# A two-layer recurrence on one core: three of layer 1's four tiles in bf16 parts, its columns in two halves, residual sums on GpSimd

## The chip, the cores and the metric

The kernel runs on one core of a Trainium2 chip. Its time is the device time of one execution in microseconds; the median of 3 runs before the change is 2182.97 us (2181.4 to 2183.67). All matrices and the input and output lie in HBM at the start and the end.

## The reference

```python
def layer(x, h0, Wx, Wh, b):              # N=8 rows, T=1024 steps, 512 columns
    xW = jnp.einsum('ntd,dh->nth', x, Wx) + b
    def step(h_prev, xw_t):
        h_next = jnp.tanh(h_prev @ Wh + xw_t)
        return (h_next, h_next)
    _, hs = jax.lax.scan(step, h0, jnp.swapaxes(xW, 0, 1))
    return jnp.swapaxes(hs, 0, 1)

x = x + layer(x, cond, L0_Wx, L0_Wh, L0_b)   # float32 throughout
x = x + layer(x, cond, L1_Wx, L1_Wh, L1_b)
```

Each layer is a chain of 1024 steps, each step a product of an 8x512 state with a 512x512 matrix, a sum with the projected input of that step, and a tanh. Layer 1 reads layer 0's output.

## The kernel before, in words

The 512 state columns are four tiles k of 128 partitions. A matmul has a state tile as its stationary operand, 32 columns wide (four steps' places of 8 rows, of which the current step's is filled and the others are zero), and 128 columns of the weight as its moving operand. The four column tiles g of the array take the four 128-column pieces of the weight, so a product with one k is a set of four matmuls, and its result stands as 32 rows per g in one PSUM bank.

Layer 0's step (recur0, L221) is 4 k x 4 g = 16 fp32 calls. Layer 1's (recur1) has two kinds of product. Tiles 2 and 3 are fp32 calls (L238). Tiles 0 and 1 (KB = 2) are exact sums of bf16 parts (L249): the weight is split once into three bf16 parts (wh_part, made on GpSimd), the state every step into three that lie in three of the tile's places (rest, L405, twice a step). The places' rows are added after the product by total1. The projections (L210) of both layers are done four steps at a time, and their 8 products per four steps are laid between the recurrences by the table PROJECT, two a step.

A step's way round: TensorE finishes a bank and increments rec_done; VectorE transposes it (turn0 L387, turn1 L391), in layer 1 also sums the places (total1 L397); ScalarE's tanh writes the new state (tanh0 L324, tanh1 L331); in layer 1 VectorE then splits it (L405). ScalarE also copies the projected input into the bank in which the next step of layer 1 accumulates (begin1, L313) and the bias into the projections' banks (L306). Layer 1 runs LAG = 8 steps behind layer 0, and in each slot TensorE does recur0, a projection, recur1, a projection. The residual sums sum_mid (L420, x plus layer 0's output, which layer 1's projection reads) and sum_out (L425) run on VectorE once in four slots.

The order of the work is the order in which each engine's program is written. VectorE's, ScalarE's, GpSimd's and SyncE's programs are unrolled over all slots. TensorE's is written as turns of RING = 8 slots: two turns unrolled (FIRST = 2), then one turn as the body of a hardware loop (Fori) of 125 passes, then three unrolled turns. Semaphores count up over groups of four slots and are set back, so that the loop's body waits for the same numbers in each pass.

Of the kernel before, what the change touches and what calls it, by code (L numbers as in the profile page):

```python
# [15 lines left out]
KB = 2  # L16
# [6 lines left out]
NG = T // S4  # L23
DMA = 16
# [3 lines left out]
WARM = 8  # L28
# [12 lines left out]
ORDER = [(l, n) for s in range(T + LAG) for l in LAYERS if (n := number(l, s)) is not None]  # L41
# [9 lines left out]
def build(nc, x, h_init, weights, out):  # L51
    ctx = ExitStack()
    with ctx:  # L53
# [3 lines left out]
        def psum(name):  # L57
            return ctx.enter_context(nc.psum_tensor(name, [P, 512], F32))
# [27 lines left out]
        ps_rec1 = [psum(f"ps_rec1_{i}") for i in range(2)]  # L86
# [40 lines left out]
        def h_count(l, n):  # L127

            s = n + LAG * l
            steps = [(m, t) for t in range(s - s % S4, s + 1) for m in LAYERS  # L130
                     if number(m, t) is not None and (m, number(m, t)) != (0, T - 1)]
            return h_done[s // S4 % 2], steps.index((l, s)) + 1

        def split_count(n):

            s = n + LAG
            return split_done[s // S4 % 2], s % S4 + 1
# [63 lines left out]
        def _(pe):  # L201
# [23 lines left out]

            def recur1(n):

                bank = ps_rec1[n % 2]  # L230
# [49 lines left out]
            for i in range(WARM):  # L280
                for bank in (*ps0, *ps_xw1, *ps_rec1):
# [20 lines left out]
        def _(act):  # L302
# [5 lines left out]
            def begin1(n):  # L308
# [4 lines left out]
                act.activation(ps_rec1[n % 2][:, 0:P], ps_xw1[c % 2][:, 0:P], ACT.Copy,  # L313
# [13 lines left out]
            def tanh1(n):  # L327
                if n % S4 == 0 and n // S4 + 1 < NG:
                    act.wait_ge(mid_done, n // S4 + 2)
                act.wait_ge(z1_done, n + 1)  # L330
                act.activation(h_of(1, n), z1[n % 2][:, :].rearrange("p (k b) -> p k b", k=KC), ACT.Tanh).then_inc(  # L331
                    h_count(1, n)[0], 1)

            def slot(s):
                last = None
                for l in LAYERS:
                    if (m := number(l, s - 1)) is not None and (l, m) != (0, T - 1):
                        last = (l, m)
# [32 lines left out]
        def _(pool):  # L371
            pool.dma_start(h_first[:, :], h_init).then_inc(s_first, DMA)
# [5 lines left out]
            pool.tensor_copy(wh_part[:, 0, :], upper(full)).then_inc(s_wpart, 1)  # L378
            pool.wait_ge(s_wrest, 1)
            pool.tensor_copy(wh_part[:, 1, :], upper(rest)).then_inc(s_wpart, 1)  # L380
            pool.tensor_tensor(wh_part[:, 2, :], rest, upper(rest), ALU.subtract).then_inc(s_wpart, 1)

        @block.vector
        def _(dve):
            def turn0(n):
                dve.wait_ge(rec_done, STEP_AT[0, n])
                dve.transpose(zt[0][n % 2][:, :], ps0[n // S4 % 2][:, 0:P]).then_inc(zt0_done, 1)  # L387

            def turn1(n):
                dve.wait_ge(rec_done, STEP_AT[1, n])  # L390
                dve.transpose(zt[1][n % 2][:, :], ps_rec1[n % 2][:, 0:P]).then_inc(zt1_done, 1)  # L391

            def total1(n):

                at = LOWEST[n % S4] * B
                dve.wait_ge(zt1_done, n + 1)
# [93 lines left out]
```

## Time and profile before

| | |
|---|---|
| median of 3 runs | 2182.97 us |
| profiled execution, its time | 2181.98 us |
| its span, first to last instruction | 2180.2 us |
| TensorE matmuls busy | 2157.1 us (99%), 90304 of them |
| VectorE busy | 1306.2 us (60%) |
| ScalarE busy | 807.7 us (37%) |
| GpSimd busy | 8.6 us (0%) |
| mean granted TensorE clock | 0.997 |

PE is TensorE's matmuls and PEld its weight loads, DVE is VectorE, ACT ScalarE, POOL GpSimd. An L number is a line of the kernel above. "issue" is idle time for which the profile shows no wait. In a view of busy time by stretch, the number behind the x in brackets counts the instructions that ran in the stretch. The granted clock is a fraction of 2.4 GHz. q1, q8 and q14 are DMA queues; those that are called "instruction" carry the engines' programs.

### The profile page before, as it was taken

The numbers are of one execution on the slowest core, as the hardware profiler recorded it, in microseconds if no ns is written. First come the engines' busy times: TensorE is split into PE (matmuls) and PEld (weight loads), VectorE is DVE, ScalarE is ACT, GpSimd is POOL, SyncE is SP. The second block draws the span as 40 slices with busy tenths as digits, with TensorE's granted clock in tenths as the row PEclk, the third lists the DMA queues.
The fourth block names the chain that finished last, engine by engine and source line by source line (L and its number), as shares of the span: only waits on it lengthen the run. The fifth ranks groups of instructions, "written<-read, shape, count | busy, mean of one in ns | idle before, by whom it ended". The sixth has DMA issues, their size and how long they took to land.

```text
span 2180.2 us, 192439 instructions
## 1 busy us (share of the span) xinstructions
PE 2157.1 (99%) x90304; PEld 2127.9 (98%) x90304; DVE 1306.2 (60%) x5643; ACT 807.7 (37%) x3585; POOL 8.6 (0%) x11
## 2 busy tenths in 40 slices
PE   7999999999999999999999999999999999999997
PEld 7999999999999999999999999999999999999997
DVE  3566666666666666666666666666666666666665
ACT  2333333333333333333333333333333333333333
POOL 1000000000000000000000000000000000000000
PEclk9999999999999999999999999999999999999999
DMA  3000000000000000000000000000000000000000
GB/s 101 23 26 22 26 22 26 22 26 22 26 22 26 22 26 22 26 22 26 22 26 22 26 22 26 22 25 23 24 23 25 23 25 23 24 24 23 25 22 17
DMA packets 112033, 55.84 MB, mean 26 GB/s; under 512 B 12448, under 2 KB 111024, under 8 KB 111536
## 3 DMA queue, kind: packets, MB, share of 16 engines
q1 hardware_dynamic: 111456, 53.53, 8.5%
q10 hardware_dynamic: 432, 1.18, 0.1%
q14 instruction: 90, 0.74, 0.1%
q8 instruction: 23, 0.38, 0.1%
q0 software_dynamic: 32, 0.02, 0.0%
HBM read 37.90 MB, written 16.78 MB: 25 GB/s over the span
## 4 chain that ended last, share of the span: by engine, by line
PE 99%; DVE 0%; DMA 0%; issue 0%; ACT 0%; SPq 0%; DVEq 0%; ACTq 0%
PE ps L221 41%; PE ps_rec L238 21%; PE ps_rec L249 16%; PE ps L210 10%; PE ps_xw L210 10%; DMA wx<-wx_in 0%; DVE zt L391 0%; DVE z L397 0%; ACT h L331 0%; DVE zt L387 0%; ACT h L324 0%; SPq L180 0%; SPq L178 0%; DVE h L405 0%; DVEq L53 0%
## 5 line engine op out<-in xcount | busy, mean ns | idle before, releaser
L221 PE MATMUL ps<-wh,h 128*32 128x128 f32 x32768 | 1089.6, 273 | 4.9 <-ACT h L324 2.8
L221 PEld LDWEIGHTS ps<-wh,h 128*32 128x32 f32 x32768 | 907.9, 110 | 22.9 <-ACT h L324 5.1
L238 PE MATMUL ps_rec<-wh,h 128*32 128x128 f32 x16384 | 638.8, 273 | 7.8 <-ACT h L331 7.1
L391 DVE STREAM_TRANSPOSE zt<-ps_rec 128x128 f32<-128x128 f32 x1024 | 324.6, 317 | 423.2 <-PE ps_rec L249 417.0
L405 DVE TENSOR_TENSOR h<-h 128x16 f32<-128x16 f32 x2050 | 359.4, 175 | 354.4 <-ACT h L331 319.1
L249 PE MATMUL ps_rec<-wh_part,h 128*32 128x128 bf16 x24576 | 534.2, 219 | 0.9 <-issue 0.8
L324 ACT ACTIVATE h<-zt 128x32 f32<-128x32 f32 x1024 | 235.1, 230 | 725.1 <-DVE zt L387 725.1
L238 PEld LDWEIGHTS ps_rec<-wh,h 128*32 128x32 f32 x16384 | 463.1, 110 | 14.8 <-ACT h L331 13.4
L331 ACT ACTIVATE h<-z 128x32 f32<-128x32 f32 x1024 | 235.1, 230 | 637.4 <-DVE z L397 637.4
L249 PEld LDWEIGHTS ps_rec<-wh_part,h 128*32 128x32 bf16 x24576 | 460.2, 97 | 2.7 <-issue 1.6
L210 PE MATMUL ps<-wx,x_pe 128*32 128x128 f32 x8192 | 414.7, 273 | 4.8 <-ACT ps L306 3.0
L210 PE MATMUL ps_xw<-wx,x_mid 128*32 128x128 f32 x8192 | 413.7, 273 | 0.0
L313 ACT ACTIVATE ps_rec<-ps_xw,mask 128x128 f32<-128x128 f32 x1024 | 330.2, 322 | 0.0
L387 DVE STREAM_TRANSPOSE zt<-ps 128x128 f32<-128x128 f32 x1024 | 316.2, 309 | 20.9 <-PE ps L221 20.9
L397 DVE TENSOR_REDUCE z<-zt 128x32 f32<-128x96 f32 x1024 | 271.7, 265 | 34.9
L210 PEld LDWEIGHTS ps<-wx,x_pe 128*32 128x32 f32 x8192 | 219.9, 110 | 6.6 <-issue 4.3
L210 PEld LDWEIGHTS ps_xw<-wx,x_mid 128*32 128x32 f32 x8192 | 220.0, 110 | 0.3 <-issue 0.3
L420 DVE TENSOR_TENSOR x_mid<-x_dve,h 128x128 f32<-128x128 f32 x256 | 74.8, 292 | 32.1 <-DVE x_out L425 7.3
L306 ACT ACTIVATE ps_xw<-bias 128x128 f32<-128x128 f32 x256 | 69.4, 271 | 0.0
L306 ACT ACTIVATE ps<-bias 128x128 f32<-128x128 f32 x256 | 67.4, 264 | 0.3
L425 DVE TENSOR_TENSOR x_out<-x_mid,h 128x128 f32<-128x128 f32 x256 | 63.9, 250 | 0.0
L283 PE MATMUL ps<-zeros 128*32 128x128 bf16 x64 | 3.1, 288 | 1.0 <-DVE zeros L444 1.0
(21 smaller groups left out, 22.7 us busy)
## 6 DMA issues: line engine op xcount, KB each, us to landing
x_pe<-x_t SPq DMA_DIRECT2D x256, 64.0 KB, 2.0
x_dve<-x_t SPq DMA_DIRECT2D x256, 64.0 KB, 2.0
out_t<-x_out SPq DMA_DIRECT2D x256, 64.0 KB, 1.5
wx<-wx_in SPq DMA_DIRECT2D x4, 256.0 KB, 8.0
wh<-wh_in ACTq DMA_DIRECT2D x1, 1024.0 KB, 8.6
wh<-wh_in SPq DMA_DIRECT2D x1, 1024.0 KB, 4.7
wx<-wx_in SPq DMA_DIRECT2D x1, 1024.0 KB, 8.2
bias<-b_in ACTq DMA_DIRECT2D x2, 64.0 KB, 4.0
```

The source lines that it names most:

```text
L210: mm = pe.matmul(rows(bank, g), src, wx[l][:, k, g * P:(g + 1) * P], start=False, stop=False, skip_group_check=True, tile_position=(0, 32 ...
L221: mm = pe.matmul(rows(ps0[n // S4 % 2], g), h_step(0, n - 1)[:, k, :], wh[0][:, k, g * P:(g + 1) * P], start=False, stop=k == KC - 1, skip ...
L238: pe.matmul(rows(bank, g), h_step(1, n - 1)[:, k, :], wh[1][:, k, g * P:(g + 1) * P], start=False, stop=False, skip_group_check=True, tile ...
L249: mm = pe.matmul(rows(bank, g), h1_bits(n - 1)[:, k, :], wh_part[:, i, at:at + P], start=False, stop=k == KB - 1 and i == PARTS - 1, skip_ ...
L306: return act.activation((ps_xw1 if l else ps0)[c % 2][:, 0:P], bias[l][:, :], ACT.Copy)
L313: act.activation(ps_rec1[n % 2][:, 0:P], ps_xw1[c % 2][:, 0:P], ACT.Copy, scale=mask[:, 32 * t:32 * t + 1]).then_inc(seed1_done, 1)
L324: act.activation(h_of(0, n), src[:, :, off:off + B], ACT.Tanh).then_inc(h_last if n == T - 1 else h_count(0, n)[0], 1)
L331: act.activation(h_of(1, n), z1[n % 2][:, :].rearrange("p (k b) -> p k b", k=KC), ACT.Tanh).then_inc(h_count(1, n)[0], 1)
L387: dve.transpose(zt[0][n % 2][:, :], ps0[n // S4 % 2][:, 0:P]).then_inc(zt0_done, 1)
L391: dve.transpose(zt[1][n % 2][:, :], ps_rec1[n % 2][:, 0:P]).then_inc(zt1_done, 1)
L397: dve.tensor_reduce(z1[n % 2][:, :].rearrange("p (k b) -> p k b", k=KC), zt[1][n % 2][:, :].rearrange("p (k r) -> p k r", r=ROWS)[:, :, at ...
L405: return dve.tensor_tensor(step[:, 0:KB, to], step[:, 0:KB, of], h1_bits(n)[:, 0:KB, of], ALU.subtract)
```

## The change

KB goes from 2 to 3: tiles 0, 1 and 2 of layer 1's recurrence are computed in bf16 parts, tile 3 alone stays fp32. Layer 1's output columns are split into two halves of 64 (HALVES), each with a PSUM bank of its own, so ps_rec1 takes two banks each and every matmul of recur1 has 64 columns. A half goes on by itself: transpose, total1 and tanh1 come twice a step, rest four times (tile 2, then tiles 0 and 1). rec_done counts layer 1's steps twice. The two residual sums go to GpSimd with waits of their own. WARM falls from 8 to 6 with eight banks in place of six.

```diff
-KB = 2
+KB = 3
...
-WARM = 8
+WARM = 6
...
-ORDER = [(l, n) for s in range(T + LAG) for l in LAYERS if (n := number(l, s)) is not None]
+HALVES = (slice(2, 4), slice(0, 2))
+IN_PARTS = (slice(2, 3), slice(0, 2))
+
+ORDER = [(l, n, i) for s in range(T + LAG) for l in LAYERS if (n := number(l, s)) is not None
+         for i in range(1 + l)]
...
-        ps_rec1 = [psum(f"ps_rec1_{i}") for i in range(2)]
+        ps_rec1 = [psum(f"ps_rec1_{i}", 2) for i in range(2)]
...
+        def rec1(n, half):
+
+            at = half.start // 2 * BANK
+            return ps_rec1[n % 2][:, at:at + HALF_P]
...
+            def whole(n, k, half):
+
+                at = half.start * ROWS
+                for g in range(QG):
+                    pe.matmul(rec1(n, half)[32 * g:32 * g + 32, :], h_step(1, n - 1)[:, k, :],
+                              wh[1][:, k, g * P + at:g * P + at + HALF_P], start=False, stop=False,
+                              skip_group_check=True, tile_position=(0, 32 * g))
+
+            def in_parts(n, k, half, stop=False):
+
+
+                for i in range(PARTS):
+                    for g in range(QG):
+                        at = k * D + g * P + half.start * ROWS
+                        mm = pe.matmul(rec1(n, half)[32 * g:32 * g + 32, :], h1_bits(n - 1)[:, k, :],
+                                       wh_part[:, i, at:at + HALF_P], start=False, stop=stop and i == PARTS - 1,
+                                       skip_group_check=True, tile_position=(0, 32 * g))
+                return mm
+
             def recur1(n):
...
-                for k in range(KB, KC):
-                    for g in range(QG):
-                        pe.matmul(rows(bank, g), h_step(1, n - 1)[:, k, :], wh[1][:, k, g * P:(g + 1) * P],
-                                  start=False, stop=False, skip_group_check=True, tile_position=(0, 32 * g))
+                for half in HALVES:
+                    whole(n, 3, half)
                 if n:
-                    pe.wait_ge(*split_count(n - 1))
+                    pe.wait_ge(*split_count(n - 1, 0))
...
-                for k in range(KB):
-                    for i in range(PARTS):
-                        for g in range(QG):
-                            at = k * D + g * P
-                            mm = pe.matmul(rows(bank, g), h1_bits(n - 1)[:, k, :], wh_part[:, i, at:at + P],
-                                           start=False, stop=k == KB - 1 and i == PARTS - 1, skip_group_check=True,
-                                           tile_position=(0, 32 * g))
-                mm.then_inc(rec_done, 1)
+                for half in HALVES:
+                    in_parts(n, 2, half)
+                if n:
+                    pe.wait_ge(*split_count(n - 1, 1))
+                for half in HALVES:
+                    in_parts(n, 0, half)
+                    in_parts(n, 1, half, True).then_inc(rec_done, 1)
...
-                act.wait_ge(z1_done, n + 1)
-                act.activation(h_of(1, n), z1[n % 2][:, :].rearrange("p (k b) -> p k b", k=KC), ACT.Tanh).then_inc(
-                    h_count(1, n)[0], 1)
+                for i, half in enumerate(HALVES):
+                    act.wait_ge(z1_done, 2 * n + i + 1)
+                    act.activation(h_of(1, n)[:, half, :],
+                                   z1[n % 2][:, :].rearrange("p (k b) -> p k b", k=KC)[:, half, :],
+                                   ACT.Tanh).then_inc(h_count(1, n, i)[0], 1)
...
+            def sum_mid(c):
+
+
+                pool.wait_ge(x_dve_loaded[c % 2], DMA * (c // 2 + 1))
+                if c >= 2:
+                    pool.wait_ge(out_done, c - 1)
+                if c == NG - 1:
+                    pool.wait_ge(h_last, 1)
+                else:
+                    pool.wait_ge(rec_done, STEP_AT[0, S4 * (c + 1), 0])
+                pool.tensor_tensor(x_group(x_mid, c), x_group(x_dve, c), h_group(0, c), ALU.add).then_inc(mid_done, 1)
+
+            def sum_out(c):
+                if c >= 2:
+                    pool.wait_ge(out_free[c % 2], DMA * (c // 2))
+                if c == NG - 1:
+                    pool.wait_ge(*h_count(1, T - 1, 1))
+                else:
+                    pool.wait_ge(rec_done, STEP_AT[1, S4 * (c + 1), 0])
+                pool.tensor_tensor(x_group(x_out, c), x_group(x_mid, c), h_group(1, c), ALU.add).then_inc(out_done, 1)
...
+            for c in range(1, NG + 2):
+                if c >= 2:
+                    sum_out(c - 2)
+                if c < NG:
+                    sum_mid(c)
...
             def turn1(n):
-                dve.wait_ge(rec_done, STEP_AT[1, n])
-                dve.transpose(zt[1][n % 2][:, :], ps_rec1[n % 2][:, 0:P]).then_inc(zt1_done, 1)
+                for i, half in enumerate(HALVES):
+                    cols = slice(half.start * ROWS, half.stop * ROWS)
+                    dve.wait_ge(rec_done, STEP_AT[1, n, i])
+                    dve.transpose(zt[1][n % 2][:, cols], rec1(n, half)).then_inc(zt1_done, 1)
...
             def split1(n):
-                dve.wait_ge(*h_count(1, n))
-                rest(n, 1).then_inc(rest_done, 1)
-                dve.wait_ge(rest_done, n + 1)
-                rest(n, 2).then_inc(split_count(n)[0], 1)
...
+                for i, tiles in enumerate(IN_PARTS):
+                    dve.wait_ge(*h_count(1, n, i))
+                    rest(n, 1, tiles).then_inc(rest_done, 1)
+                    dve.wait_ge(rest_done, 2 * n + i + 1)
+                    rest(n, 2, tiles).then_inc(split_count(n, i)[0], 1)
```

Two places where instructions move. TensorE, one step of layer 1 and the projection behind it, in the body of the loop (ps_rec is layer 1's bank, ps and ps_xw the projections' and layer 0's); before:

```order
L238 MATMUL ps_rec_1<-wh,h 32x128 [waits h_done1]
L238 MATMUL ps_rec_1<-wh,h 32x128 x7
L249 MATMUL ps_rec_1<-wh_part,h 32x128 [waits split_done1]
L249 MATMUL ps_rec_1<-wh_part,h 32x128 x23
L210 MATMUL ps_xw_0<-wx,x_mid 32x128 x4
```

The same step of the changed program:

```order
L241 MATMUL ps_rec_1<-wh,h 32x64 [waits h_done1]
L241 MATMUL ps_rec_1<-wh,h 32x64 x7
L251 MATMUL ps_rec_1<-wh_part,h 32x64 [waits split_done1]
L251 MATMUL ps_rec_1<-wh_part,h 32x64 x23
L251 MATMUL ps_rec_1<-wh_part,h 32x64 [waits split_done1]
L251 MATMUL ps_rec_1<-wh_part,h 32x64 x47
L221 MATMUL ps_xw_0<-wx,x_mid 32x128 x4
```

The 8 fp32 calls stay 8 at half the columns, the 24 bf16 calls become 72, and a second wait for the split stands among them.

VectorE, one slot in which the residual sums stood, before:

```order
L387 STREAM_TRANSPOSE zt_0<-ps_1 128x128 [waits rec_done]
L425 TENSOR_TENSOR x_out<-x_mid,h 128x4x4x8 [waits out_free0]
L420 TENSOR_TENSOR x_mid<-x_dve,h 128x4x4x8 [waits out_done,x_dve_loaded0]
L391 STREAM_TRANSPOSE zt_0<-ps_rec_0 128x128 [waits rec_done]
L397 TENSOR_REDUCE z_0<-zt_0 128x32 [waits zt1_done]
L405 TENSOR_TENSOR h<-h 128x2x8 [waits h_done1]
L405 TENSOR_TENSOR h<-h 128x2x8 [waits rest_done]
```

A slot of the changed program on VectorE:

```order
L442 STREAM_TRANSPOSE zt_0<-ps_1 128x128 [waits rec_done]
L448 STREAM_TRANSPOSE zt_0<-ps_rec_0 128x64 [waits rec_done] x2
L455 TENSOR_REDUCE z_0<-zt_0 128x16 [waits zt1_done] x2
L463 TENSOR_TENSOR h<-h 128x8 [waits h_done1]
L463 TENSOR_TENSOR h<-h 128x8 [waits rest_done]
L463 TENSOR_TENSOR h<-h 128x2x8 [waits h_done1]
L463 TENSOR_TENSOR h<-h 128x2x8 [waits rest_done]
```

The sums are gone from VectorE and stand on GpSimd, sum_out ahead of sum_mid:

```order
L419 TENSOR_TENSOR x_out<-x_mid,h 128x4x4x8 [waits rec_done,out_free1]
L410 TENSOR_TENSOR x_mid<-x_dve,h 128x4x4x8 [waits rec_done,out_done,x_dve_loaded1]
```

Layer 1's work on VectorE is four instructions before and eight now; both sums wait for rec_done on GpSimd, which they reached on VectorE by their place.

## Rows read from the trace of the kernel before

**Rows 1.** Page: busy us (share) x instructions by engine; chain that ended last, by engine.

```profile
PE 2157.1 (99%) x90304; PEld 2127.9 (98%) x90304; DVE 1306.2 (60%) x5643; ACT 807.7 (37%) x3585; POOL 8.6 (0%) x11
...
PE 99%; DVE 0%; DMA 0%; issue 0%; ACT 0%; SPq 0%; DVEq 0%; ACTq 0%
```

**Rows 2.** Chain of waits in 1000 to 1006 us: start us, us, engine, line.

```profile
1000.18 0.22 PE ps_xw L210 x8
1000.40 0.87 PE ps L221 x32
1001.27 0.22 PE ps_xw L210 x8
1001.49 0.44 PE ps_rec L238 x16
1001.93 0.34 PE ps_rec L249 x24
```

**Rows 3.** Busy time by stretch, us (x instructions): before the loop and in it.

```profile
core 0: us, PE busy (x) PEld busy (x) DVE busy (x) ACT busy (x) POOL busy (x), PEclk, DMA share, GB/s
34.86:38.58 3.72, 3.42 (x128) 3.19 (x128) 1.96 (x9) 1.39 (x7) 0.00 (x0) 1.00 0.02 4
38.58:42.60 4.02, 3.19 (x129) 2.92 (x130) 2.13 (x10) 1.07 (x5) 0.00 (x0) 1.00 0.21 55
...
61.21:64.67 3.46, 3.21 (x128) 3.03 (x128) 1.33 (x6) 1.14 (x5) 0.00 (x0) 1.00 0.11 31
1000.00:1003.73 3.73, 3.73 (x165) 3.73 (x155) 2.22 (x10) 1.15 (x5) 0.00 (x0) 1.00 0.04 12
```

**Rows 4.** Timeline of the weight loads, 33 to 68 us [idle before].

```profile
38.59 0.28 PEld L249 LDWEIGHTS ps_rec<-wh_part,h 128*32 128x32 bf16 x19 [0.54 <-issue]
...
42.59 0.47 PEld L221 LDWEIGHTS ps<-wh,h 128*32 128x32 f32 x18 [1.08 <-issue]
```

**Rows 5.** DMA queues, packets, MB, share: page; 0:28, 28:66, 66:2143, 2143:2180 us.

```profile
q8 instruction: 23, 0.38, 0.1%
...
q8 instruction: 4, 0.07, 0.9%
...
q8 instruction: 11, 0.18, 2.1%
...
q14 instruction: 87, 0.71, 0.1%
...
q8 instruction: 8, 0.13, 1.4%
```

**Rows 6.** Busy time by stretch, same columns: the loop's first pass, its middle, the end.

```profile
46.70:66.80 20.10, 18.02 (x722) 16.87 (x716) 10.35 (x44) 5.89 (x28) 0.00 (x0) 1.00 0.09 25
1000.00:2000.00 1000.00, 999.94 (x42067) 990.27 (x42057) 608.40 (x2628) 376.07 (x1672) 0.00 (x0) 1.00 0.08 24
2160.00:2180.00 20.00, 9.48 (x357) 7.28 (x356) 9.25 (x40) 3.86 (x17) 0.00 (x0) 0.89 0.04 12
```

**Rows 7.** Groups by line: line engine op names shapes xcount | busy us, mean ns | idle.

```profile
L405 DVE TENSOR_TENSOR h<-h 128x16 f32<-128x16 f32 x2050 | 359.4, 175 | 354.4 <-ACT h L331 319.1
...
L391 DVE STREAM_TRANSPOSE zt<-ps_rec 128x128 f32<-128x128 f32 x1024 | 324.6, 317 | 423.2 <-PE ps_rec L249 417.0
...
L397 DVE TENSOR_REDUCE z<-zt 128x32 f32<-128x96 f32 x1024 | 271.7, 265 | 34.9
...
L331 ACT ACTIVATE h<-z 128x32 f32<-128x32 f32 x1024 | 235.1, 230 | 637.4 <-DVE z L397 637.4
...
L420 DVE TENSOR_TENSOR x_mid<-x_dve,h 128x128 f32<-128x128 f32 x256 | 74.8, 292 | 32.1 <-DVE x_out L425 7.3
...
L377 POOL TENSOR_TENSOR wh_rest<-wh 128x1024 f32<-128x1024 f32 x1 | 1.9, 1890 | 11.2 <-DMA wh<-wh_in 11.2
...
L449 DVE MEMSET ones<- 128x8 f32 x4 | 0.1, 65 | 0.1
...
L481 POOL MEMSET const-float32-0.0<- 128x1 f32 x1 | 0.1, 98 | 0.2 <-issue 0.2
```

More of the change, by code:

```diff
@@ L23 @@
 NG = T // S4
+BANK = 512
+HALF_P = P // 2
 DMA = 16
@@ L125, in build, with h_count, split_count @@
         h_done = [sem(f"h_done{j}") for j in range(2)]
-        def h_count(l, n):
+        def h_count(l, n, i=0):
             s = n + LAG * l
-            steps = [(m, t) for t in range(s - s % S4, s + 1) for m in LAYERS
+            steps = [(m, t, j) for t in range(s - s % S4, s + 1) for m in LAYERS for j in range(1 + m)
                      if number(m, t) is not None and (m, number(m, t)) != (0, T - 1)]
-            return h_done[s // S4 % 2], steps.index((l, s)) + 1
-        def split_count(n):
+            return h_done[s // S4 % 2], steps.index((l, s, i)) + 1
+        def split_count(n, i):
             s = n + LAG
-            return split_done[s // S4 % 2], s % S4 + 1
+            return split_done[s // S4 % 2], 2 * (s % S4) + i + 1
         block = ctx.enter_context(nc.Block())
@@ L280, in _ @@
             for i in range(WARM):
-                for bank in (*ps0, *ps_xw1, *ps_rec1):
+                for bank in (*ps0, *ps_xw1, *ps_rec1, *(two[:, BANK:] for two in ps_rec1)):
                     for g in range(QG):
@@ L312, in begin1 @@
                     act.wait_ge(proj1_done, c + 1)
-                act.activation(ps_rec1[n % 2][:, 0:P], ps_xw1[c % 2][:, 0:P], ACT.Copy,
+                halves = ps_rec1[n % 2][:, :].rearrange("p (i z) -> p i z", i=2)[:, :, 0:HALF_P]
+                act.activation(halves, ps_xw1[c % 2][:, 0:P].rearrange("p (i z) -> p i z", i=2), ACT.Copy,
                                scale=mask[:, 32 * t:32 * t + 1]).then_inc(seed1_done, 1)
@@ L337, in slot @@
                     if (m := number(l, s - 1)) is not None and (l, m) != (0, T - 1):
-                        last = (l, m)
+                        last = (l, m, l)
                 if (n := number(0, s)) is not None:
@@ L378, in _ @@
             pool.tensor_copy(wh_part[:, 0, :], upper(full)).then_inc(s_wpart, 1)
+            sum_mid(0)
             pool.wait_ge(s_wrest, 1)
@@ L393, in total1 @@
             def total1(n):
                 at = LOWEST[n % S4] * B
-                dve.wait_ge(zt1_done, n + 1)
-                dve.tensor_reduce(z1[n % 2][:, :].rearrange("p (k b) -> p k b", k=KC),
-                                  zt[1][n % 2][:, :].rearrange("p (k r) -> p k r", r=ROWS)[
-                                      :, :, at:at + PARTS * B].rearrange("p k (i b) -> p k b i", b=B),
-                                  AX.X, ALU.add).then_inc(z1_done, 1)
-            def rest(n, part):
+                for i, half in enumerate(HALVES):
+                    dve.wait_ge(zt1_done, 2 * n + i + 1)
+                    dve.tensor_reduce(z1[n % 2][:, :].rearrange("p (k b) -> p k b", k=KC)[:, half, :],
+                                      zt[1][n % 2][:, :].rearrange("p (k r) -> p k r", r=ROWS)[
+                                          :, half, at:at + PARTS * B].rearrange("p k (i b) -> p k b i", b=B),
+                                      AX.X, ALU.add).then_inc(z1_done, 1)
@@ L404, in rest @@
+            def rest(n, part, tiles):
                 step, to, of = h_step(1, n), h1_cols(n, part), h1_cols(n, part - 1)
-                return dve.tensor_tensor(step[:, 0:KB, to], step[:, 0:KB, of], h1_bits(n)[:, 0:KB, of], ALU.subtract)
+                return dve.tensor_tensor(step[:, tiles, to], step[:, tiles, of], h1_bits(n)[:, tiles, of],
+                                         ALU.subtract)
             def split1(n):
-                dve.wait_ge(*h_count(1, n))
-                rest(n, 1).then_inc(rest_done, 1)
@@ L430, in slot @@
                     turn0(n)
-                if s % S4 == 0:
-                    if 0 <= (c := s // S4 - 3) < NG:
-                        sum_out(c)
-                    if 0 <= (c := s // S4 - 1) < NG:
-                        sum_mid(c)
                 if (n := number(1, s)) is not None:
@@ L456, in _ @@
             dve.wait_ge(s_hinit, 2)
-            rest(-1, 1).then_inc(s_hrest, 1)
+            rest(-1, 1, slice(0, KB)).then_inc(s_hrest, 1)
             dve.wait_ge(s_hrest, 1)
-            rest(-1, 2).then_inc(s_hsplit, 1)
-            for s in range(T + LAG + 1):
+            rest(-1, 2, slice(0, KB)).then_inc(s_hsplit, 1)
+            for s in range(T + LAG):
                 slot(s)
```

20 lines of the change are left out of this document (4 added, 16 removed).

## The prediction

> **What bounds the kernel now.** I read the page's busy line first: TensorE is busy 99% of the span, VectorE 60%, ScalarE 37% [rows 1]. The chain of waits agrees: 99% of it is TensorE, nearly all in four lines. Then one step in that chain [rows 2]: projection 0.22, layer 0's recurrence 0.87, projection 0.22, layer 1's fp32 part 0.44, its bf16 part 0.34, together 2.09 us. One fp32 call leaves two matmul records (32 for the 16 calls of layer 0), each with a weight load of its own. A step is therefore 32 + 16 + 16 + 24 = 88 matmuls and 88 loads, 176 instructions. 42067 matmuls in 1000 us [rows 6] are 478 steps, 2.092 us each, 16.74 us a pass of the eight-step loop.
>
> So far the question seems to be how many columns TensorE streams. But a third view shows a second limit, in the stretch before the loop, where TensorE's program runs straight through. There its busy time falls to 3.4 of every 3.72 to 4.02 us, and each of these windows holds 127 to 129 matmuls [rows 3], which with their loads are 256 instructions, while 3.73 us in the loop hold 165. At the border of two windows the weight loads stop for 0.5 to 1.1 us with "issue" as the reason: no semaphore, no data [rows 4]. Every 256 instructions, whatever they are, TensorE stands still. The DMA view names the cause: queue q8 moves instructions, 0.38 MB in 23 packets [rows 5], so pieces of 16 KB; one per 256 instructions makes 64 bytes an instruction. There are 4 pieces in the first 28 us, 11 from 28 to 66 us, none from 66 to 2143 us (the answer for that stretch has q14, the other engines' queue, and no q8), 8 after. TensorE executed 2 x 90304 = 180,608 instructions [rows 1], which would be 705 pieces, and 23 were read: the 125 passes of the loop run from what had been read once. Written out, the program is 2560 instructions ahead of the loop, 1408 in it and 2048 behind it, 6016 or 23.5 pieces, as counted. So a piece takes about 3.73 us to come when the engine waits for it (eight windows from 34.86 to 64.67, of which [rows 3] has three; the last is the fastest, 3.46), TensorE uses it up in 256/176 x 2.09 = 3.04 us, and it is the loop's residence that keeps 3.73 out of 2076 us of the run.
>
> The Trainium skill says of this (Runtime: NRT & Kernel Launch, Instruction fetch mechanics) that the instruction memory is refilled in 16 KiB blocks of 256 instructions, that it is a FIFO, and that TensorE's holds 128 KiB or 2048 instructions. The trace agrees on the block, and with the size in so far as 1408 fit.
>
> **The change part by part.** Layer 1's step had 8 fp32 calls and 24 bf16; it gets 8 fp32 calls of 64 columns and 72 bf16 of 64.
>
> TensorE's columns. Removed are one fp32 tile, 0.22 us, and six bf16 sets of four column tiles, 0.34/6 = 0.056 us a set. 128 columns at 2.4 GHz are 0.0533, so 0.0025 of a set are fixed. If 64 columns cost half plus this, the 18 new bf16 sets take 18 x 0.0292 = 0.53 and the four fp32 half sets 4 x 0.0558 = 0.22: 0.75 where 0.775 stood, 0.02 less a step, 25 us in 1024 steps; without the fixed part 70 us less. From the other side, if a set of 64 costs what one of 128 costs (loads are as many columns as before), it is 18 x 0.056 + 4 x 0.109 = 1.44, 0.67 more a step, 690 us. I take 0.75, because in [rows 2] time goes with columns: 8 fp32 matmuls 0.22, 16 in 0.44.
>
> The Trainium skill would have it far worse (TensorE: Matmul & The Clock Gate, "Wait — 56ns, not 53.3ns?"): start to start never under about 25 ns. By it 72 matmuls would be 1.8 us. The trace differs: 24 in 0.34 us are 14 ns each.
>
> TensorE's instructions. Each call brings its load, so a step has 32 + 16 + 16 + 72 = 136 matmuls, 272 instructions, and the loop body has 2176: 8.5 pieces, 139 KB. Both order excerpts show it: x23 and x7 become x7, x23 and x47 between the same neighbours. What was resident before is known from the trace: with its start at 2560 and the piece borders as found, the body touched 6 pieces, and the piece read ahead makes 7. The new body starts at 3328, ends at 5504, and touches 9, with the one read ahead 10. Whether 10 pieces fit is the whole question, since no row of before has a loop longer than 1408.
>
> If they don't fit, the jump back asks for the oldest piece, which the newest have overwritten, and so on round the loop: each pass reads all 9. One pass is then: 0.75 of the last piece, 0.75 x 256/272 x 2.07 = 1.5 us; the jump's target fetched with TensorE waiting, 3.73; and 8 borders at 3.73 each, 29.8. Sum 35.0 us in place of 16.74. With 3.46 for a piece it is 32.6; if the piece read ahead past the loop's end must land first, up to 2.3 more, 37.3. Outside the loop: before, 2180.2 - 125 x 16.74 = 88, which includes 3.4 that the loop's first pass lost to fetching (20.1 [rows 6] less 16.74). Eight unrolled steps ahead of it go from 5.5 to 8.5 pieces, 11.2 more; the last eight full steps from 16.7 to 31.7, 15 more; the last eight of layer 1 alone have 176 instructions each after the change, 5.5 pieces, 20.5 us, against 16.7 at most, 4 more. 88 - 3 + 30 = 115. Total 115 + 125 x 35.0 = 4490, and with the 1.8 us around the span 4492, which I round to 4500. The profiled execution took 2181.98 and the median is 2182.97, so no correction is due.
>
> Everything else hides behind 4.4 us a step, but I give the price for when it doesn't. VectorE: layer 1's transpose, its sum over the parts and the two rests (0.32 + 0.27 + 2 x 0.175 = 0.94 [rows 7]) come twice at half the size, which costs between 0.94 and 1.88; the smallest operation took 65 ns [rows 7], so four pairs add about 4 x 0.065, and I take 1.20. With layer 0's transpose of 0.32 that is 1.5 us a step, and the residual sums (0.29 each, two in four steps) leave the engine. Layer 1's chain from its last matmul to the last rest is then 0.19 + 0.33 + 0.23 + 0.48 = 1.23 us and handovers, against 1.31 + 0.22 + 0.18 until TensorE wants it. ScalarE gets a second tanh of 0.23 [rows 7]; begin1 sees the same 128 columns. GpSimd: 1024 elements took 1.89 us and one took 0.10 [rows 7], so 128 take 0.10 + 0.22 = 0.32, with 0.29 on VectorE as the low end and 0.6 as the high. sum_out now stands ahead of sum_mid in the same slot and waits for layer 1's half step, and tanh1 waits for sum_mid: 0.64 us behind that half step, against 0.19 + 0.19 + 0.17 = 0.55 until tanh1 is ready anyway, so 0 to 0.6 us once in four steps, 0 to 150 us, if the loop is resident; nothing if it isn't.
>
> With TensorE waiting 3.7 us at a jump its clock may fall: the granted clock was 0.89 of 2.4 GHz over the last 20 us, with TensorE busy half of them [rows 6]. At 1.2 GHz a piece would take 3.9 us to execute, about what it takes to come, so I add nothing and keep up to 150 us in the range.
>
> **The rivals.**
> A (forecast, 0.58): whole body fetched again each pass, 4500 us, own range 4150 to 4850 (125 x 32.6 and 37.3, with the clock). For it: a memory that held 7 pieces and needs 10; against it: no row shows a full memory. What tips it from even: after the 15 pieces up to 66 us, the last of which is the one behind the loop's end, nothing more was read in 2076 us of idle queue, as if the room were full at 7 or 8. By the 2048 instructions of the Trainium skill's page named above the body is 128 too long.
>
> B (0.23): too long, but only what overlaps is lost. If a piece sits at its number modulo 8, pieces 12 and 20, 13 and 21 displace each other and 14 to 19 stay. Each pass then waits 3.7 for piece 12, 2.3 for 13, and 1.8 for 20: 16.5 + 7.8 = 24.3 us, 3040 + 115 = 3155, range 2950 to 3450. Against it: what streams in order need not be kept by address.
>
> C (0.12): 10 pieces fit and the time is the streamed columns with a new wait: 2183 - 25 + 30 = 2188 from columns and fetching, up to 150 more from GpSimd's late sum, up to 690 from the sets. 2188 to 2870.
>
> D (0.07), not slower: 10 pieces fit, GpSimd's sum is in time and the fixed part of a set vanishes: 2183 - 70 + 30 = 2143, up to 2187. It decides as soon as columns save over 30/1024 = 0.03 us a step. For it speaks that TensorE is the chain; against it that its row must beat the 0.02 worked out above. Of its chance 0.05 is faster, 0.02 within 0.2%, about what a measurement here can tell from no change; C gives another 0.01 there.
>
> **How the numbers follow.** A has 0.58 and most of it lies under 4850; B 0.23. The range must reach from B's low end to A's high end to hold eight in ten: 2950 to 4850. Its middle is nearly empty: the time should be near 4500 or near 3200. Faster 0.05, same 0.03, slower 0.92.
>
> **What would show it.** Right: hundreds of 16 KB pieces on q8, some 9 or 10 a pass, 1125 to 1250 in the loop; TensorE busy under half of the span; in the chain "issue" as the largest part; stalls 3.7 us apart with 128 matmuls between, and VectorE, ScalarE and GpSimd idle most of the time. B would show 4 or so pieces a pass and stretches of six pieces without a stall. Wrong: fewer than 50 pieces on q8, TensorE at 99% as before, a step near 2.07 us; then the memory is larger than thought, and the halves and GpSimd's sums decide.

## The result, and the profile after

The changed kernel takes 4463.41 us (median of 4 runs, 4456.75 to 4472.42), the kernel before 2183.32 (4 runs beside them): 2.0445 times as long, 95% interval 2.0396 to 2.0493. The forecast was 4500 us.

The page of the changed kernel, its busy line, then the instruction queues, answers to [rows 1] and the first of [rows 5]:

```profile
PE 2720.1 (61%) x139456; PEld 2460.5 (55%) x139456; DVE 1597.9 (36%) x9227; ACT 948.3 (21%) x4609; POOL 243.7 (5%) x523
...
q8 instruction: 1275, 20.89, 2.0%
q14 instruction: 132, 1.08, 0.1%
```

TensorE's busy share falls from 99% to 61%, VectorE's from 60% to 36% and ScalarE's from 37% to 21%: none of them is the bound by its work. Queue q8 has 1275 pieces where it had 23. The chain of waits is no help this time: it comes out at 0% for every engine. The idle time isn't the reason, since the view also reads 0% in a kernel without it (the sums on GpSimd alone, below) and works in the padded loops that have it. So the next view is the busy time by stretch, three rows between stalls (they answer to [rows 3], same columns) and one over the middle of the run (it answers to the middle of [rows 6]):

```profile
1849.70:1853.17 3.47, 2.26 (x128) 2.11 (x128) 1.54 (x9) 1.02 (x5) 0.00 (x0) 1.00 0.02 5
1853.17:1856.64 3.47, 2.46 (x128) 2.06 (x128) 1.54 (x9) 0.78 (x4) 0.91 (x2) 1.00 0.14 40
1856.64:1860.38 3.74, 2.30 (x128) 2.13 (x128) 1.54 (x9) 0.83 (x4) 0.00 (x0) 1.00 0.09 24
1000.00:2000.00 1000.00, 614.49 (x31332) 557.44 (x31325) 359.90 (x2079) 213.47 (x1039) 52.69 (x116) 0.92 0.06 16
```

The stretches hold 128 matmuls and 128 loads each, 256 instructions, and last 3.47 or 3.74 us, TensorE being busy 2.3 to 2.5 of them. This is the pattern of [rows 3], but in the middle of the loop. 31332 matmuls in 1000 us at 136 a step are 230 steps, 4.34 us each, 34.7 us a pass. The timeline of TensorE's matmuls, most of one pass; only the pieces that begin after idle time are shown (start us, length, what, idle before):

```profile
1826.54 0.36 PE L241 MATMUL ps_rec<-wh,h 128*32 128x64 f32 x10 [1.72 <-issue]
...
1830.28 0.30 PE L221 MATMUL ps_xw<-wx,x_mid 128*32 128x128 f32 x2 [1.45 <-issue]
...
1835.75 1.08 PE L232 MATMUL ps<-wh,h 128*32 128x128 f32 x32 [4.01 <-issue]
...
1839.29 0.67 PE L251 MATMUL ps_rec<-wh_part,h 128*32 128x64 bf16 x36 [1.16 <-issue]
...
1846.23 0.59 PE L251 MATMUL ps_rec<-wh_part,h 128*32 128x64 bf16 x52 [0.74 <-issue]
...
1849.70 0.66 PE L251 MATMUL ps_rec<-wh_part,h 128*32 128x64 bf16 x60 [1.22 <-issue]
```

At 1835.75 is the jump back: 4.0 us idle ahead of the first matmul of the body. Behind it come the borders between pieces, with 0.7 to 1.7 us each. The reader is to see that the waits fall on four different lines of the program, on fp32 and bf16, recurrence and projection alike, and that each says "issue". The one regular thing is the count of instructions. The DMA view of 34.8 us, 1820.9 to 1855.7, the length of a mean pass:

```profile
q8 instruction: 10, 0.16, 2.0%
```

Ten pieces: by the count of the program, the nine that the body touches and the one read ahead at its end, which the jump makes useless. The groups that the change put in place of those of [rows 7]:

```profile
L448 DVE STREAM_TRANSPOSE zt<-ps_rec 128x64 f32<-128x64 f32 x2048 | 489.8, 250 | 1884.5 <-PE ps_rec L251 1877.7
...
L358 ACT ACTIVATE h<-z 128x16 f32<-128x16 f32 x2048 | 365.7, 214 | 1873.2 <-DVE z L455 1296.7
L463 DVE TENSOR_TENSOR h<-h 128x8 f32<-128x8 f32 (+2 forms) x4098 | 610.1, 169 | 343.2 <-ACT h L358 173.9
...
L455 DVE TENSOR_REDUCE z<-zt 128x16 f32<-128x48 f32 x2048 | 326.3, 187 | 0.8 <-DVE zt L448 0.4
...
L410 POOL TENSOR_TENSOR x_mid<-x_dve,h 128x128 f32<-128x128 f32 x256 | 116.2, 454 | 38.1 <-PE ps L232 4.5
```

Half the columns cost 250 ns where all cost 317, half the sum 187 where all cost 265, and GpSimd takes 454 ns for a residual sum that VectorE did in 292.

### The profile page after: what moved, and what is told of

Read it like the earlier page. It is cut to its first block and busy times, and to the rows that moved or that the text cites. A ratio compares the mean times of both kernels' runs of the same rounds, so it can differ in the third digit from the quotient of the medians.

```text
span 4467.0 us, 296119 instructions
## 1 busy us (share of the span) xinstructions
PE 2720.1 (61%) x139456; PEld 2460.5 (55%) x139456; DVE 1597.9 (36%) x9227; ACT 948.3 (21%) x4609; POOL 243.7 (5%) x523
## 3 DMA queue, kind: packets, MB, share of 16 engines
q8 instruction: 1275, 20.89, 2.0%
## 5 line engine op out<-in xcount | busy, mean ns | idle before, releaser
L232 PE MATMUL ps<-wh,h 128*32 128x128 f32 x32768 | 1227.3, 292 | 524.3 <-issue 521.4
L251 PE MATMUL ps_rec<-wh_part,h 128*32 128x64 bf16 x73728 | 990.5, 201 | 671.9 <-issue 669.9
L251 PEld LDWEIGHTS ps_rec<-wh_part,h 128*32 128x32 bf16 x73728 | 837.5, 99 | 757.4 <-issue 742.6
L448 DVE STREAM_TRANSPOSE zt<-ps_rec 128x64 f32<-128x64 f32 x2048 | 489.8, 250 | 1884.5 <-PE ps_rec L251 1877.7
L241 PE MATMUL ps_rec<-wh,h 128*32 128x64 f32 x16384 | 569.2, 233 | 352.4 <-issue 345.6
L358 ACT ACTIVATE h<-z 128x16 f32<-128x16 f32 x2048 | 365.7, 214 | 1873.2 <-DVE z L455 1296.7
L463 DVE TENSOR_TENSOR h<-h 128x8 f32<-128x8 f32 (+2 forms) x4098 | 610.1, 169 | 343.2 <-ACT h L358 173.9
L419 POOL TENSOR_TENSOR x_out<-x_mid,h 128x128 f32<-128x128 f32 x256 | 116.4, 455 | 4171.1 <-PE ps_rec L251 4163.4
L455 DVE TENSOR_REDUCE z<-zt 128x16 f32<-128x48 f32 x2048 | 326.3, 187 | 0.8 <-DVE zt L448 0.4
L410 POOL TENSOR_TENSOR x_mid<-x_dve,h 128x128 f32<-128x128 f32 x256 | 116.2, 454 | 38.1 <-PE ps L232 4.5
```

Of the source, the lines that this page charges most:

```text
L232: mm = pe.matmul(rows(ps0[n // S4 % 2], g), h_step(0, n - 1)[:, k, :], wh[0][:, k, g * P:(g + 1) * P], start=False, stop=k == KC - 1, skip ...
L241: pe.matmul(rec1(n, half)[32 * g:32 * g + 32, :], h_step(1, n - 1)[:, k, :], wh[1][:, k, g * P + at:g * P + at + HALF_P], start=False, sto ...
L251: mm = pe.matmul(rec1(n, half)[32 * g:32 * g + 32, :], h1_bits(n - 1)[:, k, :], wh_part[:, i, at:at + HALF_P], start=False, stop=stop and ...
L358: act.activation(h_of(1, n)[:, half, :], z1[n % 2][:, :].rearrange("p (k b) -> p k b", k=KC)[:, half, :], ACT.Tanh).then_inc(h_count(1, n, ...
L448: dve.transpose(zt[1][n % 2][:, cols], rec1(n, half)).then_inc(zt1_done, 1)
L455: dve.tensor_reduce(z1[n % 2][:, :].rearrange("p (k b) -> p k b", k=KC)[:, half, :], zt[1][n % 2][:, :].rearrange("p (k r) -> p k r", r=ROWS)[
```

## The experiments

**The length of the loop alone.** Three kernels are the kernel before, with cheap matmuls added in the body of TensorE's loop and nowhere else (18, 34 or 48 a step):

```
+            def turn(r, pads=0):
...
+                    for i in range(pads):
+                        g = i % QG
+                        pe.matmul(ps_pad[32 * g:32 * g + 32, 0:1], zeros[:, 0:ROWS], zeros[:, 0:1],
+                                  start=True, stop=True, skip_group_check=True, tile_position=(0, 32 * g))
...
             with pe.Fori(0, AFTER - FIRST, 1):
-                turn(FIRST)
+                turn(FIRST, 18)
```

18 a step, a body of 1696 instructions:

> The kernel before, with 18 one-column matmuls on zeros into a spare bank added to each of the eight steps of the loop's body: 1408 + 288 = 1696 instructions, which with the start at 2560 touch 7 pieces of 256, 8 with the piece read ahead. Theory F (fetch: TensorE's memory keeps 8 pieces, and what doesn't fit is read again each pass): still resident, 2183 plus 125 x 8 x 18 x 7 ns = 126 us at most, so 2183 to 2310, and 23 or so pieces on q8. Rival H (the halved columns and their 272 instructions a step are slow in themselves, the length of the loop doesn't matter): the same, 2183 to 2310. It only fixes one side of the border.

2327.79 us, 1.0658 times before (1.0627 to 1.0689), 24 pieces on q8. Still resident, with 8 pieces counted with the one read ahead. It lies 18 us over what was expected. 144 us for 18000 added matmuls are 8 ns each, but the pads (ps_pad) themselves take 7. TensorE at the end of a step with the jump back behind it, and at the end of the next step:

```profile
1001.46 0.29 PE L281 MATMUL ps_pad<-zeros 128*32 128x1 bf16 x18
1001.72 1.08 PE L222 MATMUL ps<-wh,h 128*32 128x128 f32 x32
...
1003.83 0.27 PE L281 MATMUL ps_pad<-zeros 128*32 128x1 bf16 x18
1003.94 1.06 PE L222 MATMUL ps<-wh,h 128*32 128x128 f32 x32
```

From the first pad to the next matmul pass 0.11 us in one case and 0.26 in the other, once in eight steps. 125 times 0.15 us are 19. So the jump back costs 0.15 us here although the loop is resident.

34 a step, 1952 instructions:

> As with 18, but 34 added matmuls a step: 1952 instructions, fewer than 2048, which touch 8 pieces, 9 with the one read ahead. Theory F with the piece read ahead counted: no longer resident, a pass is 7 borders x 3.73 + 2.1 + 4.3 = 32.5 us, 125 x 32.5 + 88 = 4150 us, and about 9 pieces a pass, 1125 on q8. Theory F2 (what counts is the body's length against 2048): resident, 2183 plus up to 240 = 2200 to 2420. Rival H: 2200 to 2420.

3992.25 us, 1.8278 times before (1.8221 to 1.8336), 1141 pieces, 9 a pass. So 16 more matmuls a step, 16000 in the run, cost 1664 us, where the first 18000 cost 144. A body of 1952 is under 2048 and doesn't fit. This is as theory F has it, which counts the piece read ahead, and F2 falls, which looks at the length against 2048. Between 1696 and 1952 no length was tried. The weight loads of one of its passes, those that begin after idle time:

```profile
1661.14 0.81 PEld L222 LDWEIGHTS ps<-wh,h 128*32 128x32 f32 x31 [1.24 <-issue]
1664.89 0.65 PEld L222 LDWEIGHTS ps<-wh,h 128*32 128x32 f32 x24 [1.22 <-issue]
...
1671.14 0.84 PEld L222 LDWEIGHTS ps<-wh,h 128*32 128x32 f32 x20 [3.86 <-issue]
```

The same two waits as in the changed kernel, 1.2 at a border and 3.9 at the jump, in a program with the old columns, banks and engines. F had 4150 us; a pass came to 31.2 us for 32.5.

48 a step, 2176 instructions, the length of the changed body:

> As before, but 48 added matmuls a step: 2176 instructions, exactly the body of the changed kernel, at the old columns, banks and engines. Theory F in both forms: 10 pieces a pass, 35 us a pass, 4400 to 4500 us, as slow as the changed kernel although layer 1, VectorE and GpSimd work as before. Rival H: 2183 plus 48 x 8 x 125 x 7 ns = 336 at most, under 2520 us.

4453.43 us, 2.039 times before (2.0331 to 2.0449), 1266 pieces. The changed kernel has 4463. With the same number of instructions, and nothing else of the change, the time is the changed kernel's within 10 us. This shows the cause: of 2280 us lost, the length of the loop's body gives all but 10. Rival H is out by 1900 us. Here the chain of waits can be followed:

```profile
PE 67%; issue 30%; DVE 2%; ACT 1%; DMA 0%; SPq 0%; DVEq 0%; ACTq 0%
```

**What a jump costs.** The changed kernel with TensorE's loop written out:

```
-            with pe.Fori(0, AFTER - FIRST, 1):
-                turn(FIRST)
-            for r in range(AFTER, END):
+            for r in range(FIRST, END):
```

> The changed kernel with TensorE's loop written out: the same matmuls in the same order, 281,000 instructions in a straight line, 1098 pieces. Theory F: the pieces come one after the other at 3.73 us without a jump, 1098 x 3.73 = 4095 us, so 370 us less than with the loop, which is 3 us a jump. Rival H, or a jump that costs nothing: 4463 us, the same. If pieces in a row come faster when there is no jump, down to 3.46: 3800 us.

4072.21 us, 1.8644 times before (1.8567 to 1.8722), with 1089 pieces: 4063.4 us of span over 1089 is 3.73 a piece, as in the stretch ahead of the loop in [rows 3]. The 391 us to the changed kernel are 3.1 us for each of 125 jumps. Its middle, beside the changed kernel's above:

```profile
1000.00:2000.00 1000.00, 622.63 (x34579) 564.10 (x34583) 399.23 (x2288) 234.03 (x1144) 58.14 (x128) 1.00 0.06 17
```

The granted clock is 1.00 here and 0.92 on the mean there. So waits of 1 to 2 us leave it at 2.4 GHz, and it falls to 1.2 for a while behind the 4 us jumps. The changed kernel from one jump on:

```profile
1831.50:1835.75 4.25, 0.24 (x8) 0.00 (x0) 1.17 (x8) 0.37 (x2) 0.00 (x0) 1.00 0.02 4
1835.75:1839.29 3.54, 2.38 (x93) 2.23 (x93) 0.32 (x1) 0.66 (x3) 0.00 (x0) 0.64 0.02 5
1839.29:1842.70 3.41, 3.41 (x100) 3.37 (x103) 1.65 (x9) 0.51 (x4) 0.90 (x2) 0.50 0.11 30
1846.20:1849.70 3.50, 2.25 (x128) 2.13 (x128) 1.54 (x9) 1.03 (x5) 0.00 (x0) 1.00 0.02 5
```

At the low clock TensorE is busy without a break (3.41 of 3.41 us). The two pieces from 1839.29 to 1846.23 still take 6.94 us, 3.47 each as at 2.4 GHz. In this pass the clock costs nothing that can be seen. Over the whole run, the two kernels don't tell its cost from that of the wait.

Two turns a pass, half the jumps:

```
-            with pe.Fori(0, AFTER - FIRST, 1):
+            with pe.Fori(0, (AFTER - FIRST) // 2, 1):
                 turn(FIRST)
-            for r in range(AFTER, END):
+                turn(FIRST + 1)
+            for r in range(AFTER - 1, END):
```

> The changed kernel with two turns (16 steps, 4352 instructions) in the loop's body and half the passes, 62. Theory F: every border costs what it did, half the jumps go; the straight line of the same program took 4072 us and the loop of 125 jumps 4463, 3.1 us a jump, so 63 jumps less save 197 us: 4266 us, and one of the two pieces that a jump throws away goes too, about 1275 - 63 x 1.5 = 1180 pieces. If the cost went with the body's length instead (a longer loop, more to read), it would stay at 4463.

4271.82 us, 1.9565 times before (1.9526 to 1.9604), 1150 pieces. 6 us from the expected 4266. The pieces are 30 fewer than expected: 125 less than in the changed kernel are two for each of 63 jumps saved, and I had counted one and a half. A body twice as long is faster than the one that only just overflows. Once a loop doesn't fit, its length no longer matters, only the instructions that are read and the jumps.

**The parts of the change in a resident loop.** These all keep TensorE's body at 1408 to 1600 instructions. KB = 3 at the full 128 columns, one bank, sums on VectorE:

```
-KB = 2
+KB = 3
```

> The kernel before with KB = 3 alone: tiles 0 to 2 in bf16 parts at the full 128 columns in one bank, sums on VectorE. A step has 92 matmuls, the body 1472 instructions, 8 pieces with the one read ahead, so resident by the fetch theory. Theory S (streamed columns bound a resident loop): one fp32 tile less (0.218) and three bf16 sets more (3 x 0.056), 0.051 us less a step: 2183 - 52 = 2131 us. Rival L (layer 1's chain is late, since TensorE now wants the split 0.22 us earlier, at 1.53 us after the last matmul where it stood ready at about 1.34 and costs some ns more for 24 elements): 0.05 to 0.1 us of wait a step, 2180 to 2230 us.

2224.39 us, 1.0184 times before (1.0167 to 1.0201), slower. The waits name the reason (engine, tile, line, waited for; us in total, times, longest):

```profile
PEld ps_rec L249 <- DVE h L405: 160.9, 885, 0.3
```

TensorE's weight loads wait for the split of the state in 885 steps, 0.18 us each, which they never had to before. Theory L holds and S falls in this form: if the columns save their 52 us, the chain takes them and 40 more.

The sums on GpSimd alone (the first lines leave VectorE's program, the last stand in GpSimd's):

```
-                if s % S4 == 0:
-                    if 0 <= (c := s // S4 - 3) < NG:
-                        sum_out(c)
-                    if 0 <= (c := s // S4 - 1) < NG:
-                        sum_mid(c)
...
+            for c in range(1, NG + 2):
+                if c >= 2:
+                    sum_out(c - 2)
+                if c < NG:
+                    sum_mid(c)
```

> The kernel before with the two residual sums on GpSimd alone, with the changed kernel's waits and order. GpSimd's two sums took 0.455 us each in the changed kernel, and sum_out waits for layer 1's step. Theory W (tanh1 waits for sum_mid once in four steps): sum_mid ends about 1.0 us after layer 1's last matmul where tanh1 could start at 0.65, so tanh1 comes 0.35 to 0.4 us late in 256 slots, of which TensorE feels about 0.1: 2183 + 25 to 50 = 2210 to 2230 us. Rival V (VectorE's 0.54 us in four slots delayed something): 2183 - 14 = 2169 us. No difference if the wait is hidden: 2183.

2283.52 us, 1.0455 times before (1.0438 to 1.0472): theory W, twice to four times as large as expected. The timeline of one such slot:

```profile
999.99 0.45 POOL L390 TENSOR_TENSOR x_out<-x_mid,h 128x128 f32<-128x128 f32 x1 [7.75 <-PE ps_rec L249]
...
1000.24 0.26 DVE L423 TENSOR_REDUCE z<-zt 128x32 f32<-128x96 f32 x1
...
1000.58 0.45 POOL L381 TENSOR_TENSOR x_mid<-x_dve,h 128x128 f32<-128x128 f32 x1
...
1001.07 0.23 ACT L331 ACTIVATE h<-z 128x32 f32<-128x32 f32 x1 [1.11 <-POOL x_mid L381]
...
1001.34 0.38 PEld L238 LDWEIGHTS ps_rec<-wh,h 128*32 128x32 f32 x16 [0.46 <-ACT h L331]
```

Between the two sums pass 0.14 us more for the hand-over, so the pair takes 1.04 us from start to end. VectorE's sum over the parts was done at 1000.50, and tanh1 starts at 1001.07. I had let TensorE feel only 0.1 of the delay; its loads stop for 0.46, and 256 x 0.39 is the 99 us.

Both together:

> KB = 3 at full width and the sums on GpSimd together. Theory W on top of S: the split is then wanted 0.22 us earlier and comes 0.35 to 0.4 late in one slot of four, 0.3 us x 256 = 77 us: 2131 + 77 = 2208 us. Rival V: 2131 - 14 = 2117 us.

2339.2 us, 1.0713 times before (1.0695 to 1.0731). The wait is again mis-sized, by the same reason: 115 us on top of KB = 3.

A set of 64 columns, on one of the two bf16 tiles:

```
-                    for i in range(PARTS):
-                        for g in range(QG):
-                            at = k * D + g * P
-                            mm = pe.matmul(rows(bank, g), h1_bits(n - 1)[:, k, :], wh_part[:, i, at:at + P],
...
+                    for cols in ((slice(0, 64), slice(64, P)) if k == 0 else (slice(0, P),)):
+                        for i in range(PARTS):
+                            for g in range(QG):
+                                at = k * D + g * P
+                                mm = pe.matmul(rows(bank, g)[:, cols], h1_bits(n - 1)[:, k, :],
+                                               wh_part[:, i, at + cols.start:at + cols.stop],
```

> The kernel before with the 12 bf16 matmuls of tile 0 cut into 24 of 64 columns in the same bank: 1600 instructions in the body, resident by the fetch theory. Theory S: a set of four at 64 columns takes half a set of 128 and the fixed 2.5 ns, so three more fixed parts, 0.0075 us a step, 8 us: 2191. In the changed kernel's trace the sets of 64 stand 28 to 36 ns apart, mean about 31, where half is 27.9: by that 6 x 31 - 3 x 56 = 18 ns a step, 19 us: 2202. Rival H (a set of 64 costs what one of 128 costs): 3 x 56 ns more a step, 172 us: 2355.

2211.72 us, 1.0131 times before (1.0114 to 1.0148), 26 pieces. Its middle, at 100 matmuls a step:

```profile
1000.00:2000.00 1000.00, 1000.00 (x47346) 986.15 (x47340) 605.15 (x2605) 373.10 (x1656) 0.00 (x0) 1.00 0.08 24
```

473.5 steps in 1000 us are 2.112 us each, 20 ns more than the 2.092 of [rows 6]. It is tempting to divide this by the sets (31 ns for one of 64, the mean distance in the changed kernel), but most of it isn't theirs. TensorE in two steps, with the jump back between 1003.39 and 1003.74:

```profile
1000.96 0.55 PE L250 MATMUL ps_rec<-wh_part,h 128*32 128x64 bf16 x36
1001.30 0.42 PE L210 MATMUL ps_xw<-wx,x_mid 128*32 128x128 f32 x8
1001.52 1.08 PE L221 MATMUL ps<-wh,h 128*32 128x128 f32 x32
...
1003.39 0.42 PE L210 MATMUL ps<-wx,x_pe 128*32 128x128 f32 x8
1003.74 1.08 PE L221 MATMUL ps<-wh,h 128*32 128x128 f32 x32
```

The 36 bf16 matmuls take 0.34 us from their start to the next line's. By the starts of some 800 such steps in the trace (300 to 2000 us) it is 342.5 ns, where the 24 of the kernel before take 335.0. So six sets of 64 for three of 128 cost 7.5 ns, and a set of 64 takes 29.2: theory S, to the digit. The projection in front of the jump takes 0.35 us to the next line, 0.22 elsewhere. Once in eight steps this is 0.13, and 0.03 in the kernel before, which makes 12 ns a step. The other 8 us of the 28 lie outside the loop: 20 ns in 1000 steps are only 20 us. Rival H falls here too. Why this body's jump costs more than that of the kernel before isn't shown.

Whether 29.2 holds for the 72 bf16 matmuls that the changed kernel has in a step, not 24, is another matter. In the straight-line kernel I find one step in which they run at 2.4 GHz without a wait between:

```profile
28.67 0.78 PE L251 MATMUL ps_rec<-wh_part,h 128*32 128x64 bf16 x72
29.26 0.32 PE L221 MATMUL ps<-wx,x_pe 128*32 128x128 f32 x3
```

0.59 us for 18 sets are 33 ns each, the first six at 29 and the last ten at 33 or 34. By this one sample the columns would give back nothing: 0.06 us more than the 0.53 that I took, for the 0.02 that they were to save.

**A version that beats both.** If the chain is what KB = 3 lacks, the passing on by halves should be had without halving TensorE's matmuls. First the rests alone, in two pieces, and tile 2 multiplied first:

```
-                rest(n, 1).then_inc(rest_done, 1)
-                dve.wait_ge(rest_done, n + 1)
-                rest(n, 2).then_inc(split_count(n)[0], 1)
+                for tiles in IN_PARTS:
+                    rest(n, 1, tiles).then_inc(rest_done, 1)
+                for i, tiles in enumerate(IN_PARTS):
+                    dve.wait_ge(rest_done, 2 * n + i + 1)
+                    rest(n, 2, tiles).then_inc(split_count(n, i)[0], 1)
```

> KB = 3 at full width (2224 us), with the rests cut in two, tile 2 first, in the order part 1 of tile 2, part 1 of tiles 0 and 1, part 2 of tile 2, part 2 of tiles 0 and 1, and TensorE multiplying tile 2 first behind a wait of its own. Theory L (the split's lateness is the loss): TensorE stood 0.16 us a step for the split; tile 2's alone ends 0.02 to 0.03 us sooner (169 and 184 ns an operation), the other hides behind its 0.17 us of matmuls: 25 to 30 us less, 2195 to 2200. If it needs the second wait too, VectorE's four operations cost 0.1 more than two: 2224 to 2300. It beats the kernel before (2184) only if the wait falls by 0.04 a step.

2187.65 us (10 runs), 1.002 times before (1.0011 to 1.003): 7 us under the expected range, and no gain. Then the sum over the parts and the tanh in halves too:

```
+                for i, half in enumerate(HALVES):
+                    act.wait_ge(z1_done, 2 * n + i + 1)
+                    act.activation(h_of(1, n)[:, half, :],
+                                   z1[n % 2][:, :].rearrange("p (k b) -> p k b", k=KC)[:, half, :],
+                                   ACT.Tanh).then_inc(h_count(1, n, i)[0], 1)
...
+                for half in HALVES:
+                    dve.tensor_reduce(z1[n % 2][:, :].rearrange("p (k b) -> p k b", k=KC)[:, half, :],
...
+                for i, tiles in enumerate(IN_PARTS):
+                    dve.wait_ge(*h_count(1, n, i))
+                    rest(n, 1, tiles).then_inc(rest_done, 1)
```

> The kernel of the cut rests (KB = 3 at full width, 2188 us), with layer 1's sum over the parts and its tanh in two halves as well, tiles 2 and 3 first; TensorE's matmuls and their 128 columns stay, so 1472 instructions in the body. It takes over the changed kernel's passing on by halves where it costs TensorE no instruction. In the changed kernel the half sum took 187 ns and the half tanh 214, against 265 and 230 whole: tile 2's and 3's state is there 0.09 us sooner, and the second tanh hides behind the first. Theory L (layer 1's chain is what keeps KB = 3 from its column time): the step falls from 2.094 us towards the 2.031 of the columns, by 0.04 to 0.06: 2125 to 2150 us, faster than the kernel before by 1.5 to 2.5%. Rival (VectorE's added instructions, now 10 a step, make layer 0's transpose late or the second half's split is the last): 2180 to 2210.

2144.71 us (5 runs, 2143.59 to 2147.43), 0.9822 times before (0.9808 to 0.9835): faster than the kernel before by 1.8%. Its middle, 92 matmuls a step, then a slot of its ScalarE and VectorE:

```profile
1000.00:2000.00 1000.00, 999.90 (x44868) 955.42 (x44864) 712.59 (x4144) 432.46 (x2194) 0.00 (x0) 1.00 0.09 24
```

```profile
1003.23 0.33 DVE L405 TENSOR_REDUCE z<-zt 128x16 f32<-128x48 f32 x2
...
1003.48 0.33 ACT L337 ACTIVATE h<-z 128x16 f32<-128x16 f32 x2 [0.30 <-DVE z L405]
...
1003.73 0.50 DVE L413 TENSOR_TENSOR h<-h 128x8 f32<-128x8 f32 x4 [0.17 <-ACT h L337]
```

487.7 steps in 1000 us, 2.050 each on the mean. That is 0.02 over the 2.031 that the columns alone would take (2.082 between undisturbed steps of the kernel before, less 0.051). Two half sums take 0.33 us together and two half tanhs 0.33, though one is listed with 204 and 211 ns here: the second runs partly beside the first. So cutting them shortens the way to the first half and costs little.

## Why the prediction was right

The forecast case was the one that came: 4463 for 4500, inside its own range of 4150 to 4850.

- *The step of the instruction count* held to the piece. 2176 instructions in the body, 9 pieces touched, one read ahead: 10 a pass. The range given was 1125 to 1250 in the loop, and 1275 less some 25 outside it are 1250. The count from the program (2560, 1408, 2048) was worth more here than any duration.
- *3.73 us a piece* held: 4063.4 / 1089 in the straight line. A pass came to 34.8 us from jump to jump on the mean (34.7 by the matmuls counted) for 35.0 worked out, the jump's wait to 4.0 us for 3.73.
- *Whether 10 pieces fit* was the open point, and I gave it 0.81 of no with one row to go by. The pads place the border: 8 with the one read ahead stay, 9 don't. That nothing more was read after 66 us was a sign and not a proof. The Trainium skill's 2048 instructions (Runtime: NRT & Kernel Launch, Instruction fetch mechanics) are 8 pieces, which agrees with the runs; but a body of 1952 fell out, so for a loop 7 pieces is the usable length, as far as these two bodies show.
- *Rival B*, only what overlaps is read again, is refuted: it had some 4 pieces a pass and 3155 us. All 9 are read, and the one ahead.
- *Rivals C and D* never got their turn, since nothing was resident. Their parts can be held against the experiments. GpSimd's sum was taken at 0.32 us and took 0.45; its order and waits were put at 0 to 150 us, and alone they cost 99. A bf16 set of 64 columns was taken at 29.2 ns, in D at 26.7: it costs 29.2 in runs of 24 matmuls and 33 in the one undisturbed run of 72. So D's condition, that the columns save over 0.03 us a step, isn't met, though no run has the whole change in a resident loop. (The sum for D has a slip too: without the fixed part the sets are 0.48 + 0.21 us, 84 us less in all and not 70.) In C, VectorE's half operations are listed nearer to whole ones (250 of 317, 187 of 265, 169 of 175 ns) than the 0.065 added to a pair. Their lengths add up to 0.31 + 0.50 + 0.37 + 0.68 = 1.86 us a step, but they overlap: the page's busy time is 1597.9 us over 1024 steps, 1.56 for the 1.5 I took.
- *The allowance for the clock*, up to 150 us, was not needed. The granted clock fell to 0.92 in the loop. In the piece behind the jump TensorE had no time over (3.41 of 3.41 us), but the two pieces together were no later.
- *Two signs that I named did not come.* TensorE was to be busy under half of the span, and shows 61%: a stretch of 128 matmuls reads as 2.3 to 2.5 us busy, where its share of a step, 1.95, was reckoned, and at the low clock it reads as busy throughout. "Issue" was to be the largest part of the chain: the view gave nothing for the changed kernel, and in the loop with 48 pads it is 30% beside TensorE's 67%. The mechanism rests on the count of pieces and the padded loops, not on these.

What remains open is what the whole change would do in a resident loop. No run has it: its 272 instructions a step need a body of four steps, which the ring of eight would not allow as written. KB = 3 in full columns, the sums on GpSimd and six half sets, each alone, cost 40, 99 and 28 us, the last mostly outside the sets; that they add up was tried only for the first two (155 for 139).

## What to carry to other kernels

Count the instructions of a loop's body, loads included, before counting its columns. In these runs TensorE kept eight pieces of 256 instructions, one of them the piece read ahead. A body that needed a ninth ran at 3.7 us a piece and 3 us a jump, as long as the work of a piece was shorter than that: a body of 1696 instructions cost 144 us for its pads and one of 1952 cost 1808. And before a small difference is divided by the matmuls that were changed, look at the jump: 12 of 20 ns a step stood there. A finer grain that halves matmuls doubles their instructions; the same grain on the engines behind them (sum and tanh in halves) took the wait out of KB = 3 at full columns and gave 1.8%.

## What the runs showed that I had not expected

- A loop of 1952 instructions, which touches 8 pieces, is too long, though 2048 would be 8 pieces. 9 pieces are fetched a pass, so the one behind the loop's end is among them; that it displaces the first is how I read it.
- A loop that doesn't fit is slower than the same program written out, 4463 to 4072 us, and a body twice as long sits between them at 4272.
- Two operations with 16 results per partition in a row, independent of each other, end 0.33 us after the first began on both VectorE and ScalarE, though each is listed with 204 or 211 ns.
